# Gates of the experts brought to all partitions by DMA through DRAM, and gating in other slots

## The reference

```python
x = x + attn_a(layernorm(x))
x = x + ffn(layernorm(x))
x = x + attn_b(layernorm(x))
x = x + ffn(layernorm(x))

def ffn(x):                               # 4096 tokens, 8 experts, 2 for each token
    scores = softmax(x @ gate_w.T)
    top_scores, sel = top_k(scores, 2)
    routed_in = x[token] * top_score      # the gate scales the expert's input
    ...
    h = silu(xe @ w1[e]) * (xe @ w3[e])
    out_routed += where(m, h @ w2[e], 0)
    ...
    return silu(x @ w1s) * (x @ w3s) @ w2s + out_routed   # and a shared expert
```

## Time and profile before

| | |
|---|---|
| Time, median of 3 runs | 1005.57 us (1003.54 to 1006.71) |
| Profiled execution, its own time | 1006.98 us |
| its span in the trace | 1005.2 us |
| Granted TensorE clock, mean | 0.98 |
| Busy: TensorE, DVE, ACT, POOL | 87%, 72%, 58%, 52% of the span |
| Attention A and setup, about | 0 to 270 us |
| First feed-forward layer, about | 270 to 490 us |
| Attention B, about | 490 to 785 us |
| Second feed-forward layer, about | 785 to 1005 us |

### The profile page before, as it was taken

One profiled execution on the slowest core, in us unless ns is written; L12 is line 12 of the kernel. 1 busy time (PEld: TensorE's weight loads), 2 busy tenths in 40 slices (PEclk: granted clock), 3 DMA queues, 4 the chain that ended last, 5 costly groups with the idle time before them and its releaser, 6 DMA issues.

```text
span 1005.2 us, 22245 instructions
## 1 busy us (share of the span) xinstructions
PE 872.4 (87%) x7264; PEld 619.6 (62%) x7264; DVE 727.7 (72%) x1970; ACT 578.4 (58%) x905; POOL 524.0 (52%) x606
## 2 busy tenths in 40 slices
PE   0498989887899999999979888888887799999998
PEld 0245555544488778777745555555544588787887
DVE  4357767776677787776678899898884577777765
ACT  1177777766644444344478888888885344444443
POOL 2556666657145555543445657575733554545541
PEclk9999999999899999999889999999997899999999
DMA  8000000000000000000000000000000000000000
GB/s 231 0 2 2 0 0 0 0 1 2 2 1 1 1 1 1 0 0 2 0 1 2 2 0 0 0 0 0 1 1 1 1 12 11 11 2 10 10 11 22
DMA packets 14591, 8.70 MB, mean 9 GB/s; under 512 B 1600, under 2 KB 14144, under 8 KB 14528
## 3 DMA queue, kind: packets, MB, share of 16 engines
q1 hardware_dynamic: 12944, 7.28, 2.6%
q10 hardware_dynamic: 1584, 0.62, 0.2%
HBM read 5.80 MB, written 2.10 MB: 8 GB/s over the span
## 4 chain that ended last, share of the span: by engine, by line
PE 20%; issue 13%; DVE 11%; POOL 7%; ACT 2%; DVEq 0%; POOLq 0%; ACTq 0%
DVE s_qs L1032 6%; PE psum L763 5%; PE psum L731 4%; POOL f_xe_lo L1378 3%; POOL f_p L1388 3%; PE psum L1271 2%; PE psum L713 2%; PE psum L1233 1%; DVE f_xe L1415 1%; PE psum L829 1%; PE psum L1235 1%; PE psum L1234 1%; PE psum L818 1%; PE psum L748 1%; ACT f_xe_hi L1347 1%
## 5 line engine op out<-in xcount | busy, mean ns | idle before, releaser
L1347 ACT ACTIVATE f_xe_hi<-f_xe 128x512 fp32r<-128x512 f32 x128 | 80.9, 632 | 204.8 <-DVE f_xe L1415 204.8
L1032 DVE TENSOR_REDUCE s_qs<-psum 128x4 fp32r<-128x1024 f32 x128 | 156.3, 1222 | 35.5 <-PE psum L748 34.7
L1378 POOL TENSOR_TENSOR f_xe_lo<-f_xe,f_xe_hi 128x512 fp32r<-128x512 f32 x64 | 83.9, 1312 | 185.0 <-ACT f_xe_hi L1347 185.0
L1271 PEld LDWEIGHTS psum<-w,f_h 128*128 128x128 f32 x1152 | 147.7, 191 | 8.7
L1271 PE MATMUL psum<-w,f_h 128*128 128x128 f32 x1152 | 153.0, 276 | 0.0
L414 ACT ACTIVATE s_probs<-psum 128x1024 f32<-128x1024 f32 x128 | 125.6, 1024 | 32.7 <-PE psum L301 32.2
L899 ACT ACTIVATE s_probs<-psum 128x1024 f32<-128x1024 f32 x128 | 131.2, 1025 | 19.5 <-PE psum L731 17.8
L1233 PE MATMUL psum<-f_xe_hi,w_hi 128*128 128x512 f32 x288 | 127.0, 441 | 7.7 <-POOL f_xe_lo L1378 7.1
L1431 DVE TENSOR_TENSOR f_h<-psum,f_g 128x512 f32<-128x512 f32 x144 | 99.1, 689 | 45.0 <-ACT f_g L1332 34.7
L1235 PE MATMUL psum<-f_xe_lo,w_hi 128*128 128x512 f32 x288 | 114.1, 396 | 0.0
L1234 PE MATMUL psum<-f_xe_hi,w_lo 128*128 128x512 f32 x288 | 113.6, 394 | 0.0
(11 more groups left out here) (179 smaller groups left out, 1747.3 us busy)
## 6 DMA issues: line engine op xcount, KB each, us to landing
x<-in_x SPq DMA_DIRECT2D x4, 512.0 KB, 9.2
out<-x SPq DMA_DIRECT2D x8, 256.0 KB, 2.3
w<-in_w SPq DMA_DIRECT2D x3, 512.0 KB, 7.0
select_raw<-in_select SPq DMA_DIRECT2D x1, 512.0 KB, 4.9
rope_cos<-in_rope_cos SPq DMA_DIRECT2D x1, 256.0 KB, 3.6
rope_sin<-in_rope_sin SPq DMA_DIRECT2D x1, 256.0 KB, 4.4
wqkv_a<-in_Wqkv_aT ACTq DMA_DIRECT2D x1, 192.0 KB, 6.8
bqkv<-in_bqkv ACTq DMA_DIRECT2D x1, 192.0 KB, 7.5
```

The lines of the kernel that those rows point to most:

```text
L1032: dve.tensor_reduce(o[:, r:r + 2, 2 * p:2 * p + 2, 24:25].bitcast(F32R), room(km, i).rearrange("p (r j s) -> p r j s", r=2, j=2), AX.X, AL ...
L1271: ins = pe.matmul(Y[k % 2][:, t * P:(t + 1) * P], g.f_h[:, q, t * P:(t + 1) * P], g.w2[:, e, :], start=(e == 0 and t == 0), stop=(e == NE ...
L1378: pool.tensor_tensor(xe_lo[:, ring(e), :], src, xe_hi[:, ring(e), :], ALU.subtract).then_inc(xe_lo_pool.sem, 1)
```

## The change

The product with `select`, the transposes of the gates and the buffers `f_ss` and `f_st` are gone. `gates` now ends with one DVE transpose in blocks of 32 x 32 of the 128 x 32 gates into `f_sg`. SP writes `f_sg` to a scratch buffer in DRAM (two of them, 8 x 512 values, by turns), waits until it has landed, and reads each expert's row of 512 gates back to all 128 partitions, into a ring `f_gt` of four; the transfers for experts 4 to 7 wait until the ring's place has been read. `scale` reads both its inputs from SBUF. SP also issues the second layer's stores of x, each after the fourth broadcast of a chunk two later.

The gating stands in other slots, x transposes and logits now for a chunk two steps ahead. POOL makes seven of the nine low parts of a chunk, DVE those of experts 3 and 4.

```diff
-LOW_ON_DVE = (2, 5, 6, 7)
+LOW_ON_DVE = (3, 4)
-LEAD = {1: (0,), 3: (1,), 4: (2,), 6: (3,), 8: (4,), 9: (5,), 13: (6,), 15: (7,)}
+LEAD = {0: (0,), 2: (1,), 3: (2,), 5: (3,), 6: (4,), 7: (5,), 13: (6,), 15: (7,)}
 FF = {
-    "norm": 8, "x_turn": 0, "xt_sb": 0, "logits": 1, "best": 1, "pow": (2, 2, 2, 2), "gates": 5, "s_turn": 6,
-    "st_sb": 6, "residual": 0, "rstd": 0,
+    "norm": 5, "x_turn": 7, "xt_sb": 7, "logits": 8, "best": 0, "pow": (0, 0, 0, 0), "gates": 3, "residual": 6, "rstd": 6,
 }
+    def turned(n, k, e, task):
+
+        return ([(n + 1, k + 1)] if k == -1 and e == FF_LEAD[task] else []) + (
+            [(n + 2, k + 2)] if k + 2 < NCH and e == FF[task] else [])
...
-                pe.matmul(SB, g.select[:, e, :], st[:, km % 2, :],
-                          start=True, stop=True).then_inc(sb_mm.sem, 1)
...
-            def s_turn():
-                pe.wait_ge(lo_sb.sem, lo_sb.upto(n + 1))
-                for t in range(4):
-                    ins = pe.transpose(T[:, t * P:(t + 1) * P], ssp[:, t, :], g.identity[:])
-                ins.then_inc(st_mm.sem, 1)
...
             def scale(m, km, e):
-                dve.wait_ge(sb_mm.sem, sb_mm.upto(m, e + 1))
+                dve.wait_ge(xt_sb.sem, xt_sb.upto(m))
+                dve.wait_ge(gt_sb[e % 4].sem, gt_sb[e % 4].upto(m, 16 * (e // 4 + 1)))
...
-                dve.tensor_tensor(xe[:, e % 2, :], SB, xt[:, km % 2, :], ALU.mult).then_inc(xe_sb.sem, 1)
+                dve.tensor_tensor(xe[:, e % 2, :], gt[:, e % 4, :], xt[:, km % 2, :], ALU.mult).then_inc(xe_sb.sem, 1)
...
-                dve.wait_ge(st_mm.sem, st_mm.upto(n))
-                dve.tensor_copy(ssp[:, :, 0:E].bitcast(F32R), g.f_m[:, 0, :, :]).then_inc(hi_sb.sem, 1)
-                dve.wait_ge(hi_sb.sem, hi_sb.upto(n + 1))
-                dve.tensor_tensor(ssp[:, :, E:2 * E], g.f_m[:, 0, :, :], ssp[:, :, 0:E], ALU.subtract).then_inc(lo_sb.sem, 1)
+                dve.wait_ge(written.sem, written.upto(n))
+                dve.transpose(g.f_sg[:], g.f_m[:, 0, :, :].rearrange("p t e -> p (t e)")).then_inc(sg_sb.sem, 1)
...
+        for m in range(NCH):
+            n = Step(None, 0, m)
+            sp.wait_ge(sg_sb.sem, sg_sb.upto(n))
+            sp.dma_start(g.gates[m % 2].rearrange("e (t b j) -> b (e t) j", t=4, b=4),
+                         g.f_sg[:]).then_inc(written.sem, 16)
+            sp.wait_ge(written.sem, written.upto(n))
+            for e in range(E):
+                if e >= 4 or m > 0:
+                    sp.wait_ge(xe_sb.sem, xe_sb.upto(n, e - 3) if e >= 4 else xe_sb.upto(n - 1, e + 5))
+                sp.dma_start(gt[:, e % 4, :], g.gates[m % 2, e].partition_broadcast(P)).then_inc(gt_sb[e % 4].sem, 16)
+                if not first and e == 3 and m >= 2:
+                    store(m - 2)
```

More of the change, by code:

```diff
@@ L804, in x_turn @@
                 if km == 0:
[L805 removed]
+                    pe.wait_ge(before.lg_sb.sem, before.lg_sb.upto(Step(None, 0, NCH - 1)))
                 else:
@@ L1215, in body @@
         def body(n, k, part=range(E + 1)):
[L1216 to L1228, removed]
-                pe.matmul(SB, g.select[:, e, :], st[:, km % 2, :],
-                          start=True, stop=True).then_inc(sb_mm.sem, 1)
+            run = 0 <= k < NCH
             def thrice(dst, w_hi, w_lo, x_hi, x_lo):
@@ L1302, in body @@
                     up(m, km, next_e)
-                for m, km, next_e in ahead(n, k, e, 3):
-                    if next_e not in (0, E):
-                        spread(m, km, next_e)
-                if gate and e == AT["x_turn"]:
-                    x_turn()
-                if gate and e == AT["logits"]:
-                    logits()
-                if gate and e == AT["s_turn"]:
-                    s_turn()
+                for m, km in turned(n, k, e, "x_turn"):
+                    x_turn(m, km)
+                for m, km in turned(n, k, e, "logits"):
+                    logits(m, km)
                 if run:
                     down(e)
-                for m, km, next_e in ahead(n, k, e, 3):
-                    if next_e == 0:
-                        spread(m, km, next_e)
         return body
@@ L1535, in sync, with store @@
     def sync(sp):
-        view = out.rearrange("(n s) (c p) d -> n p (s c) d", s=2, p=P)
-        with sp.Fori(0, NCH) as n:
-            sp.wait_ge(x_sb.sem, x_sb.upto(Step(n, 1, 0)))
-            sp.dma_start(view[n], g.x[:, :, :].rearrange("p (n c) d -> p n c d", c=4)[:, n, :, :]
-                         ).then_inc(stored, 16)
-        sp.wait_ge(stored, 16 * NCH)
+        def store(m):
+            view = out.rearrange("(n s) (c p) d -> n p (s c) d", s=2, p=P)
+            sp.wait_ge(x_sb.sem, x_sb.upto(Step(None, 0, m)))
+            sp.dma_start(view[m], g.x[:, 4 * m:4 * m + 4, :]).then_inc(stored, 16)
+        for m in range(NCH):
[10 more added lines that the diff above has]
+                    store(m - 2)
+        if not first:
+            for m in (NCH - 2, NCH - 1):
+                store(m)
+            sp.wait_ge(stored, 16 * NCH)
     layer = Shared()
     layer.tensor, layer.scalar, layer.gpsimd, layer.vector, layer.sync = tensor, scalar, gpsimd, vector, sync
-    layer.st_sb, layer.xe_sb, layer.h_sb, layer.x_sb, layer.rstd_sb = st_sb, xe_sb, h_sb, x_sb, rstd_sb
+    layer.lg_sb, layer.h_sb, layer.x_sb, layer.rstd_sb = lg_sb, h_sb, x_sb, rstd_sb
     return layer
@@ L1646, in program @@
         g.f_xn, g.f_xt = sb("f_xn", [P, 4, DIM]), sb("f_xt", [P, 2, CH])
-        g.f_ss, g.f_st = sb("f_ss", [P, 4, P]), sb("f_st", [P, 2, CH], F32R)
+        g.f_gt, g.f_sg = sb("f_gt", [P, 4, CH]), sb("f_sg", [P, 4 * E])
+        g.gates = nc.dram_tensor("gates", (2, E, CH), F32).ap()
         g.f_xe, g.f_g, g.f_h = (sb(x, [P, 2, CH]) for x in ("f_xe", "f_g", "f_h"))
@@ L1687, in constants @@
     identity = np.eye(P, dtype=np.float32)
-    select = np.zeros((P, E, P), np.float32)
-    for e in range(E):
-        select[e, e, :] = 1.0
-        select[E + e, e, :] = 1.0
     iota = np.tile(np.arange(E, dtype=np.float32), (P, 1))
```

55 lines of the change are left out of this document (23 added, 32 removed).

## The result

The changed kernel takes 1037.56 us (median of 4 runs, 1035.26 to 1041.23), the kernel before 1005.16 beside it (4 runs, 1003.54 to 1006.71). The ratio is 1.032, with a 95% interval of 1.030 to 1.035: 32 us slower, where 996 us and faster were forecast. The profiled execution took 1041.23 us, its span 1039.4; it is the slowest of the four, 3.7 above their median.

The account below looks back on a forecast made before the run. TensorE's queue was taken as the bound, with a DVE loop of 2.59 us a slot just below. Gains of 2.4 (first layer), 6.2 (second) and 0.9 (lead-in), 9.5 us, took 1005.57 to 996; range 983 to 1008.

Parts of the forecast that it names:

- rival B: Gate write and broadcast too long: slower beyond 6.8 us together; at 7.5 us, 20 us back, 1016; chance 0.12.
- the margin: Between DVE transpose and `xe(0)`: 6.1 us available, transfers taken as 4.8 (2.3 write, 2.5 read), hidden with 1.3 to spare.
- The estimate of 4.6: Two transfers in series, 256 KB in the second, at about 2 us fixed cost each: 4.6 us, leaving the sum unchanged.
- the logits wait: Slot 8: logits wait for `xt` over 1 us in the first layer alone; slot 4.5 us there, 3.4 in the second.
- slots 2 and 5 to 7: First-layer step: slot 2 bound by the DVE loop at 2.59 us; slots 5, 6, 7 at 2.75, 2.35, 2.75.
- `up(5)` waits behind the power and low part 5: Slot 3: TensorE idle 1.4 us before `up(5)`, behind POOL.
- Now low 5 is POOL's and ends at 10.8 + 1.3 = 12.1: Power of 6.44 us keeps POOL busy until 10.8, low part 5 follows; slot 3 is 3.8 us, 1.45 waiting.
- 27.1: First-layer step summed over nine slots, us, against 27.24 before; the second layer's step 26.0 against 26.75.
- rival C: Port holds dearer: `xe` blocked by POOL's low parts or power pieces; 12 us, 1003 to 1009, or about 1018; chance 0.15.
- step 0 of the second layer: First feed-forward step of the second layer, put down as gaining 0.7 us.
- the 9.5 of forecast gain: Whole gain in us: first layer 2.4, second layer 6.2, lead-in of the second layer 0.9.
- 1.1, 1.7 and 0.9: Gains in us: step 6 of the first layer, step 6 of the second, lead-in of the second layer.

Follow-up runs that it names:

- e1: Changed kernel with the power back in slot 2, low parts 2, 5, 6, 7 on DVE and gates in slot 4: 1066.4 us, ratio 1.056.
- e4: Changed kernel, but in step 0 of the second layer alone the power starts in slot 2 and gates stand in slot 5: 1040.9 us, ratio 1.032.
- e12: Changed kernel plus one dummy matmul in each of the eight former product places, steps 1 to 6: 1030.7 us, ratio 1.023.
- e3: The filler kernel: changed kernel plus eight matmuls into an unused bank ahead of `up(5)`, steps 1 to 6: 1025.8 us, ratio 1.017.
- e5: Changed kernel with the low part of expert 5 also on DVE (3, 4, 5), power still in slot 0: 1009.7 us, ratio 1.000.
- e2: Changed kernel with select products and gate transposes put back, its slots and low-part table kept, no transfer of gates: 1034.1 us, ratio 1.025.
- e6: The winning order: changed kernel with low parts 4, 5, 7 on DVE and the power in slot 1 behind low part 3: 1002.2 us, ratio 0.994.

## Why the prediction was wrong

**What was right.** Products, transposes and their wait are gone; transfers are no cost in the steps (rival B is out). But the margin was thinner than I had it. Where `xe(0)` waited for its transfer, in this and the other kernels with the path, it started 5.2 to 6.1 us behind the end of the DVE transpose. I had 4.8. The estimate of 4.6 taken from the Trainium skill, DMA: Bandwidth & Descriptors, Anatomy of one DMA, rests on a section that is about transfers issued by GpSimd, while SP issues these. Further: the logits wait 1.2 us in the first layer and 0.5 at most in the second; slots 2 and 5 to 7 are right to 0.1; `up(5)` waits behind the power and low part 5, at the place named. And the step of 26.6 / 25.3 that the winning order has shows that the gain sought was there.

**Step that failed first: "Now low 5 is POOL's and ends at 10.8 + 1.3 = 12.1", slot 3 = 3.8.** It measured 4.80. Two terms were charged at nothing. The power takes 6.88 us: its third piece begins 0.11 us behind a low part of DVE, both of whose inputs lie in SBUF, and lasts 2.07 us instead of 1.64. In the changed kernel 12 of the 56 pieces begin so and all 12 take 2.07 to 2.08; the other 44 take 1.63 to 1.64. I had read in the earlier trace rows that a DVE low part inside a power piece isn't held, which is right, and concluded that there was no price; the other direction, a piece that begins inside a DVE row, I hadn't asked for. Before, the pieces happened to fall elsewhere: one of 56 began beside such a row, 0.18 us before its end, and took 1.67. The second term is the same hold on low part 5 by `xe`, which reads SBUF twice now: 1.73 us in place of 1.26. With the products, where `xe` reads PSUM and starts at the same place, it is 1.26. Together 0.44 + 0.47 a step, so 27.1 becomes 28.0 and 26.0 becomes 26.9, which is what the filler kernel has, 28.1 / 26.9.

Of rival C, `xe` blocked by POOL, little is seen in the changed kernel: the median is 682 ns, and 12 of 128 take 0.77 to 0.87 us, all of them begun 0.2 to 0.3 us before a low part of POOL ends; POOL blocked by DVE is its mirror image, and it costs 12 × 0.9 = 11 us. The Trainium skill, SBUF — State Buffer, Who interferes with whom, names the pair, a DVE instruction with two SBUF inputs against a GpSimd instruction that reads SBUF. The traces agree when DVE is first; when the power is first, the DVE row kept its 0.69 us.

**Step left out: the clock.** Every slot was costed at 2.4 GHz, since the steady steps before had 1.00. The change took work from TensorE and added idle time at one place. The clock of the two stretches is from one traced execution of each kernel, the last column from all of its executions (e1 to e4 on one chip, where the kernel before had 0.966 to 0.981):

| kernel | less TensorE work | wait at `up(5)`, us | granted clock, two stretches | over the span, each execution |
|---|---|---|---|---|
| the change | yes | 2.23 | 0.94, 0.95 | 0.942 to 0.953 |
| e4, the same rows in these steps | yes | 2.23 | 0.96, 1.00 | 0.945 to 0.956 |
| e1 | yes | about 4.1, at `up(7)` | 0.93, 0.92 | 0.936 to 0.942 |
| e12, dummy products | refilled | 2.01 | 0.98, 0.99 | 0.957 to 0.966 |
| e3, wait filled | yes | filled | 0.98, 1.00 | 0.958 to 0.970 |
| e5, low part 5 on DVE | yes | 0.03 | 0.99, 1.00 | 0.959 to 0.968 |
| e2, products | no | 1.55 | 1.00, 1.00 | 0.963 to 0.976 |

Filling the wait, removing it and giving back the work each raise the clock over the span above every execution of the changed kernel. That much is shown. Which of the two counts, the lost work or the long wait, is not: no kernel has all of the old work and a wait of 2.2 us. And neither sets the clock for certain, since the same rows lost it behind eight waits of twelve in one execution and three in another.

Its price is the mean step against one that ran at 2.4 GHz throughout, 28.05 / 26.9 in e4: five steps of each layer, 5 × (29.6 − 28.05) + 5 × (27.8 − 26.9) = 12 us in the traced execution, and about 5 in that of e4. Dummy products lengthen a step at 2.4 GHz by 0.3 us at most (28.07 / 27.2 in e12), so they give back more than they cost.

**Step charged wrongly: step 0 of the second layer.** I gave it a gain of 0.7 us; it lost 8.6. In this step the power, from 818.79 for 6.44 us as shown above, sits ahead of attention rows on POOL. Timeline of the changed kernel:

```profile
826.00 0.61 POOL L980 TENSOR_TENSOR s_sq<-s_a 128x256 f32<-128x256 f32 x1
...
826.64 0.42 DVE L1073 TENSOR_REDUCE s_ms<-s_sq 128x16 f32<-128x256 f32 x1 [7.26 <-POOL s_sq L980]
...
827.18 0.68 DVE L1386 TENSOR_TENSOR f_xe_lo<-f_xe,f_xe_hi 128x512 fp32r<-128x512 f32 x1
...
827.92 0.80 PE L1218 MATMUL psum<-f_xe_hi,w_hi 128*128 128x512 f32 x1 [8.34 <-DVE f_xe_lo L1386]
```

Attention's `s_a` and `s_sq` wait for the power on POOL, its mean square on DVE for them, low part 3 of the feed forward for that in DVE's order, and TensorE for low part 3. I had followed both queues within the steady step and not in the step where another layer's rows stand between.

**The sum.** Forecast 996, measured 1037.6, 41.6 off; between the two traced executions it is 34.2 and the 9.5 of forecast gain, 43.7. Holds 11, clock in the steps 12, step 0 of the second layer 8.6 + 0.7 = 9.3: 32. The 12 are those of the slowest execution, so for the median they are likely less. The remaining 9 to 12 lie outside these steps: the stretches there are 2.2, 3.0 and 3.7 us longer, and gains of 3.7 that I had put there (1.1, 1.7 and 0.9) did not come. Outside the two stretches of steady steps the mean clocks of both whole spans (0.942 over 1039.4 us, 0.980 over 1005.2) leave 2 × 0.058 × 1039.4 − 23 − 14 = 84 us at 1.2 GHz against 40 before; that this is the cause was not tried, and it stays open; e5 has a span clock of 0.96 too and runs at par. So does why the winning order has 0.959 to 0.972 over its span where the kernel before has 0.98 in its trace.

## What to carry to other kernels

Before a long instruction is moved on an in-order queue, list what will stand behind it on that queue in every kind of step, also where two layers overlap, and give exactly those rows to another engine; the same 6.9 us cost 32 us or nothing by one number in a table. After removing matmuls look at the granted clock of the steps, in more than one execution: here it fell behind waits of 2.2 us in up to eight steps of twelve, and matmuls that compute nothing gave back more than they cost. When a rule of contention has two directions, look in the trace for both before charging nothing.

## What the runs showed that I had not expected

A POOL piece that begins while DVE runs a row with two SBUF inputs lasts 2.07 us in place of 1.64, and one that begins 0.11 us behind a row that reads PSUM, as in the kernel before, keeps 1.64; all 56 of the changed kernel follow this, if a row with under 0.3 us left to run is not counted. The other way round, 26 `xe` and 14 low parts of DVE that began inside a piece of the power kept 0.68 or 0.69 us, while in e6 an `xe` that began 1.1 us before the end of a POOL low part took 1.65. One power over 32 columns takes 5.43 us, four over 8 columns 6.44. Eight matmuls a step that compute nothing made the kernel 12 us faster in one place, and 7 us spread over the step, by the medians. And the broadcasts, 2 MB a step and 67 to 101 GB/s in the stretches of steady steps, slowed nothing that could be seen.
